# Six steps' banks and one eviction count in each word of TensorE's building table, with its waits at every sixth step

## The reference

```python
h = relu(layernorm(x)); x = x + attention(h)   # clip(qk[dst].qk[src]/8), softmax over dst, sum of v[src]
h = relu(layernorm(x)); x = x + conv(h)        # norm * segment_sum((h*norm)[src], dst) @ W + b
h = relu(layernorm(x)); x = x + edge_mlp(h)    # mlp([h[src], h[dst], edge_attr]) both ways, segment sums, mlp
h = relu(layernorm(x))
for _ in range(4):                             # x = x + the last feat
    a = segment_sum((einsum(feat, W) + b)[edge_type, src], dst); feat = gru_cell(a, feat)
```

## Time and profile before

| | |
|---|---|
| time, median of 3 runs | 13652.0 us (13648.86 to 13652.0) |
| profiled execution | 13654.69 us, its span 13653.0 us |
| busy share of the span | PE 81%, PEld 47%, DVE 41%, ACT 26%, POOL 32% |
| mean granted clock of TensorE | 0.892 |
| building, first to last matmul of L1139 | 317.0 to 2652.4 us |
| line L1139 on the chain that ended last | 11% of the span |
| L1139, 4859 matmuls | busy 1893.7 us, idle before 428.4 us, "issue" 212.9 of it |

### The profile page before, as it was taken

The page is one execution under the profiler, slowest core; times in us unless marked ns, Lnnn a source line. Parts: engine busy times, 40 slices in busy tenths (PEclk is TensorE's granted clock), DMA queues, the critical chain, the costliest instruction groups (busy, mean ns, idle before and its releaser), DMA issues.

```text
span 13653.0 us, 258090 instructions
## 1 busy us (share of the span) xinstructions
PE 11057.9 (81%) x60251; PEld 6361.4 (47%) x60252; DVE 5587.9 (41%) x21367; ACT 3529.7 (26%) x9549; POOL 4391.0 (32%) x3429
## 2 busy tenths in 40 slices
PE   2888888799976777777777777775899999999999
PEld 2444444333345555555555555554644444444443
DVE  6888888766624443443443443443311111111111
ACT  0666666533302222222222222222100000000000
POOL 2000000000005888888888888886000000000000
PEclk7666666699988999999999999998599999999999
DMA  2444444422262333333333333335399899899898
GB/s 99 139 136 139 139 136 140 139 87 93 87 273 36 42 42 42 42 42 42 42 42 42 42 42 42 42 42 35 109 354 348 338 348 348 337 349 348 338 349 306
DMA packets 1120492, 2096.55 MB, mean 154 GB/s; under 512 B 373090, under 2 KB 982915, under 8 KB 1012532
## 3 DMA queue, kind: packets, MB, share of 16 engines
q1 hardware_dynamic: 823768, 1913.47, 39.3%
q0 software_dynamic: 295904, 174.34, 12.0%
HBM read 1630.21 MB, written 457.17 MB: 153 GB/s over the span
## 4 chain that ended last, share of the span: by engine, by line
PE 54%; issue 19%; POOL 16%; DVE 4%; DMA 2%; ACT 1%; POOLq 1%; SPq 1%; DVEq 0%; ACTq 0%; another core or an unknown queue 0%
PE ps L1491 16%; PE ps L1139 11%; PE ps L1496 9%; POOL G L499 8%; POOL reverse L824 8%; PE ps L1194 4%; PE ps L1185 2%; DMA reverse<-SD,sidx 2%; DVE hots L1824 1%; PE ps L1294 1%; PE ps L1343 1%; PE ps L1354 1%; PE ps L1344 1%; POOLq L823 1%; PE ps L1357 1%
## 5 line engine op out<-in xcount | busy, mean ns | idle before, releaser
L824 POOL DMA_INDIRECT reverse<-SD,sidx x1660 | 2650.9, 1597 | 556.4 <-issue 496.2
L1491 PE MATMUL ps<-chunk,feat 128*128 128x512 f16 (+1 forms) x10192 | 2278.9, 375 | 14.8 <-DVE feat L2186 13.9
L499 POOL DMA_INDIRECT G<-h_table,idx x1660 | 1647.4, 992 | 1942.9 <-issue 1935.5
L1139 PE MATMUL ps<-hots 128*128 128x392 f16 x4859 | 1893.7, 449 | 428.4 <-issue 212.9
L1354 PE MATMUL ps<-MS,OH 128*128 128x128 f32 x3320 | 774.4, 316 | 1218.2 <-issue 811.9
L2023 DVE TENSOR_TENSOR acc<-acc,ps 128x132 f32 x1660 | 485.1, 292 | 3009.7 <-PE ps L1357 2958.5
L854 ACT ACTIVATE stagebuf<-ps 128x392 f32 x3248 | 1470.5, 506 | 884.5 <-PE ps L1142 804.8
L1491 PEld LDWEIGHTS ps<-chunk,feat 128*128 128x128 bf16 x10192 | 943.4, 98 | 1301.2 <-issue 307.8
L931 ACT ACTIVATE SD<-ps 128x129 f32<-128x129 f32 x1660 | 461.9, 278 | 3726.4 <-DMA reverse<-SD,sidx 3700.5
L1354 PEld LDWEIGHTS ps<-MS,OH 128*128 128x128 f32 x3320 | 542.8, 198 | 1771.6 <-issue 1748.7
L1343 PE MATMUL ps<-early,OT 128*128 128x256 f32 x3320 | 1081.3, 409 | 250.9 <-issue 225.8
(11 more groups left out here) (417 smaller groups left out, 14865.9 us busy)
## 6 DMA issues: line engine op xcount, KB each, us to landing
chunk<-adj SPq DMA_DIRECT2D x720, 1792.0 KB, 9.0
adj<-stagebuf SPq DMA_DIRECT2D x406, 784.0 KB, 5.3
chunkA<-adj SPq DMA_DIRECT2D x48, 1792.0 KB, 6.8
chunk<-adj SPq DMA_DIRECT2D x60, 1232.0 KB, 6.5
G<-in_edge SPq DMA_DIRECT2D x1660, 32.0 KB
G<-h_table,idx POOLq DMA_INDIRECT x1660
reverse<-SD,sidx POOLq DMA_INDIRECT x1660
reverse<-acc SPq DMA_DIRECT2D x4, 3225.0 KB, 20.0
```

The lines of the kernel that those rows point to most:

```text
L499: nc.gpsimd.indirect_dma_start(G[:, j, 0:width], None, table, bass.IndirectOffsetOnAxis(idx[:, j:j + 1], 0))\
L824: nc.gpsimd.indirect_dma_start(reverse[j % R], bass.IndirectOffsetOnAxis(sidx[:, j:j + 1], 0), SD[:, j % R, :], None, compute_op=ALU.add). ...
L1139: nc.tensor.matmul(ps[:, bass.ds(window % 8 * 512, 2 * COMBS)], hots[:, j // HG % HRING, 0:P, j % HG], hots[:, j // HG % HRING, P:P + 2 * ...
L1491: nc.tensor.matmul(bank[k % 2][:, 0:cols], feat[0][:, hi, 0:2, :].rearrange("p a d -> p (a d)"), columns(chunk4, i % DRING, m, cols), star ...
```

## The change

A word of the table now holds six steps' banks (18 bits) and above them one count of evictions (12 bits). A sweep of 64 steps has 11 words, ten of six steps and one of four, where it had 16. The table is 836 words long instead of 1216, and the words of sweep `it` begin at word 11 x `it` instead of 16 x `it`. TensorE's waits stand at every sixth step (before the steps 0, 6, ... 60 of a sweep) instead of at every fourth; the last group of a sweep has four steps. VectorE packs the new words in 15 operations. SyncE stores them with one transfer instead of two.

```diff
-VIRTW, BATCH = 16, 4
-PACK = 8
+VIRTW, BATCH = 16, 6
+BANKBITS = 3 * BATCH
...
-SWEEPW = 2 * SWEEP // PACK
+SWEEPW = -(-SWEEP // BATCH)
+WHOLE = SWEEP // BATCH
...
                 if j % BATCH == 0:
-                    free, odd = held["words"][SWEEPW // 2 + j // PACK], j // BATCH % 2
-                    pe.wait_ge(hot_made, min((k + BATCH) // HG, HGROUPS) if known(k) else it * (SWEEP // HG) + (j + BATCH) // HG)
-                    pe.wait_ge(evicted, (free >> 12) & 4095 if odd else free & 4095)
-                window = held["words"][j // PACK] >> 3 * (j % PACK)
+                    ready = min(j + BATCH, SWEEP)
+                    pe.wait_ge(hot_made, min((k - j + ready) // HG, HGROUPS) if known(k) else it * (SWEEP // HG) + ready // HG)
+                    pe.wait_ge(evicted, (held["words"][j // BATCH] >> BANKBITS) & 4095)
+                window = held["words"][j // BATCH] >> 3 * (j % BATCH)
...
-            link(copy_(pack_free, turned_free[:, :, BATCH - 1]))
-            link(both_(out=pack_free, in0=turned_free[:, :, PACK - 1], scalar=4096.0, in1=pack_free, op0=ALU.mult, op1=ALU.add))
-            link(copy_(pack_bank, turned_bank[:, :, 0]))
-            for i in range(1, PACK):
-                link(both_(out=pack_bank, in0=turned_bank[:, :, i], scalar=float(8 ** i), in1=pack_bank, op0=ALU.mult, op1=ALU.add))
...
+            copy_(need_word[:, :, 0:WHOLE], of_needed[:, :, :, BATCH - 1])
+            link(copy_(need_word[:, :, WHOLE], needed[:, :, SWEEP - 1]))
+            link(scalar_(need_word, need_word, BANKBITS, None, ALU.logical_shift_left))
+            copy_(word, of_banks[:, :, :, 0])
+            link(copy_(rest_word, banks[:, :, WHOLE * BATCH]))
+            for i in range(1, BATCH):
+                link(both_(out=word, in0=of_banks[:, :, :, i], scalar=float(8 ** i), in1=word, op0=ALU.mult, op1=ALU.add))
...
+            link(copy_(bank_word, packed[0:BC, :, :]))
+            tensor_(bank_word, bank_word, need_word, ALU.bitwise_or).then_inc(tab_copied, 1)
```

More of the change, by code:

```diff
@@ L179, in build @@
         key_table = dram("key_table", (TP, 3 * P))
-        step_rows = dram("step_rows", (BC, SWEEPS, 2, SWEEPW // 2), I32)
+        step_rows = dram("step_rows", (BC, SWEEPS * SWEEPW), I32)
         virt_rows = dram("virt_rows", (3 * VC, P), I32)
@@ L247, in build @@
         tabcols = here("tabcols", [P, 3 * BC])
-        packed = here("packed", [P, P // PACK])
+        packed = here("packed", [P, SWEEPS, SWEEPW])
         tabi = here("tabi", [P, P], I32)
@@ L611, in table @@
                 sp.dma_start(rows, tabi[0:rows.shape[0], :]).then_inc(tab_stored, 16)
-                sp.wait_ge(tab_stored, 16 * (n + 2))
+                sp.wait_ge(tab_stored, 16 * (n + 1))
                 lines = rows.rearrange("(q c) p -> q (c p)", q=count)
@@ L617, in _ @@
             sp.wait_ge(tab_copied, 1)
[L618 to L622, removed]
+            sp.dma_start(step_rows, tabi[0:BC, 0:SWEEPS * SWEEPW]).then_inc(tab_stored, 16)
+            sp.wait_ge(tab_stored, 16)
+            sp.dma_start(steptab[0:1, :], step_rows.rearrange("(o c) w -> o (c w)", o=1)).then_inc(tab_loaded, 16)
             table(1, virt_rows, 3, virttab, 32)
@@ L1126, in words @@
                     steptab[0:1, it * SWEEPW:(it + 1) * SWEEPW] if known(it) else steptab[0:1, bass.ds(it * SWEEPW, SWEEPW)],
-                    engines=(pe.engine,), min_val=0, max_val=max(8 ** PACK - 1, (VW + 8) * 4097),
+                    engines=(pe.engine,), min_val=0, max_val=(VW + PRE + 1 << BANKBITS) - 1,
                     skip_runtime_bounds_check_because="the path's tables are made of counts within these bounds")
@@ L1705, in _ @@
             v.wait_ge(tab_turned, 1)
-            turned_free, turned_bank = (bank[7][row:row + BC, 0:P].rearrange("c (w i) -> c w i", i=PACK) for row in (0, BROW))
-            pack_free, pack_bank = packed[0:BC, :], packed[BROW:BROW + BC, :]
-            link(copy_(pack_free, turned_free[:, :, BATCH - 1]))
-            link(both_(out=pack_free, in0=turned_free[:, :, PACK - 1], scalar=4096.0, in1=pack_free, op0=ALU.mult, op1=ALU.add))
-            link(copy_(pack_bank, turned_bank[:, :, 0]))
-            for i in range(1, PACK):
-                link(both_(out=pack_bank, in0=turned_bank[:, :, i], scalar=float(8 ** i), in1=pack_bank, op0=ALU.mult, op1=ALU.add))
-            link(copy_(tabi[0:BC, 0:P // PACK], pack_free))
-            copy_(tabi[BROW:BROW + BC, 0:P // PACK], pack_bank).then_inc(tab_copied, 1)
+            needed, banks = (bank[7][row:row + BC, 0:P].rearrange("c (s e) -> c s e", s=SWEEPS) for row in (0, BROW))
+            whole, last = slice(0, WHOLE * BATCH), SWEEP - WHOLE * BATCH
+            of_banks = banks[:, :, whole].rearrange("c s (w i) -> c s w i", i=BATCH)
+            of_needed = needed[:, :, whole].rearrange("c s (w i) -> c s w i", i=BATCH)
+            word, rest_word = packed[0:BC, :, 0:WHOLE], packed[0:BC, :, WHOLE]
+            bank_word = tabi[0:BC, 0:SWEEPS * SWEEPW].rearrange("c (s w) -> c s w", s=SWEEPS)
+            need_word = tabi[0:BC, P // 2:P // 2 + SWEEPS * SWEEPW].rearrange("c (s w) -> c s w", s=SWEEPS)
+            copy_(need_word[:, :, 0:WHOLE], of_needed[:, :, :, BATCH - 1])
[5 more added lines that the diff above has]
+                link(both_(out=word, in0=of_banks[:, :, :, i], scalar=float(8 ** i), in1=word, op0=ALU.mult, op1=ALU.add))
+            for i in range(1, last):
+                link(both_(out=rest_word, in0=banks[:, :, WHOLE * BATCH + i], scalar=float(8 ** i), in1=rest_word, op0=ALU.mult,
+                           op1=ALU.add))
+            link(copy_(bank_word, packed[0:BC, :, :]))
+            tensor_(bank_word, bank_word, need_word, ALU.bitwise_or).then_inc(tab_copied, 1)
             v.wait_ge(cmp_used, 3 * CG)
@@ L1759, in _ @@
             v.wait_ge(tab_turned, 2)
-            v.wait_ge(tab_stored, 32)
+            v.wait_ge(tab_stored, 16)
             copy_(tabi[0:3 * VC, :], bank[7][0:3 * VC, 0:P]).then_inc(tab_copied, 1)
@@ L1791, in _ @@
             v.wait_ge(tab_turned, 3)
-            v.wait_ge(tab_stored, 48)
+            v.wait_ge(tab_stored, 32)
             copy_(tabi[0:6, :], bank[7][0:6, 0:P]).then_inc(tab_copied, 1)
```

## The result

| | before | changed |
|---|---|---|
| time, median of 4 runs | 13652.0 us (13648.86 to 13658.5) | 13765.26 us (13754.72 to 13768.92) |
| ratio to before | | 1.008, 95% interval 1.0068 to 1.0093 |
| profiled execution, span | 13654.69 us, 13653.0 | 13754.72 us, 13753.0 |
| building, first to last matmul | 317.0 to 2652.4 us | 315.9 to 2759.3 us |

The changed kernel is 113 us slower, 0.8%. The forecast was 13867 us, 215 us slower: the sign and the cause came out as forecast, the size at half.

What follows compares the result with a forecast made beforehand. The prediction took TensorE's instruction sequencer, not its arithmetic, to bound the building. Its terms 4 + 198 + 12 + 1 gave +215 us on 13654.7, so 13870, forecast as 13867 us for the median; range 13660 to 13920.

Steps and rivals of the forecast that it cites:

- B: Rival on the table load: single words up to a 16-byte multiple, then fours; 5 accesses every sweep, 13705 us; chance 0.27.
- A: The forecast's own reading of the table load: fours only if it begins at a 16-byte multiple; 13820 to 13920 us; chance 0.50.
- Term 1: Group heads and inner steps in the building: fewer heads save 182 us, more and slower inner steps cost 185; +4 us.
- bits and place: Whether inner-step address instructions go by bits left above (heads and steps +4 us) or place in the group (-36 us).
- Term 2: TensorE's table load once a sweep: 9.5 accesses in the mean, 5.5 more than before, over 76 sweeps; +198 us.
- 1.9 for four accesses: Mean time in us taken for one table load of the kernel before, during the building; 0.475 us an access.
- 5.5 x 0.475: Table load's growth: 5.5 added accesses a sweep at the mean price of 0.475 us, 2.61 us a sweep.
- Term 3: TensorE's waits for evictions at every sixth step: 8 us over the last 112 windows, 4 in the body; +12 us.
- Term 4: Setup: VectorE's packing chain grows from 12 to 15 operations, SyncE's single store stays hidden; +1 us.
- C: Rival on the table load: price by started fours or nearly the same whatever its words; 13633 to 13665 us; chance 0.13.
- D: Rival on the table load: price by the word, five fewer save 45 us; 13624 us, or 13584; chance 0.08.
- about 200 ns a register: Skill page's price for the table load: five registers fewer save an estimated 1.0 us a sweep, -76 us; 13593 us.

Runs made afterwards that it cites:

- the single loads: Changed kernel with 14 kinds of table load, three of each, ahead of its building: eight words 0.591 us from a multiple of four, 1.941 from one past it.

## Why the prediction was right in sign and off in size

**The time.** 13765 us lies between B's 13705 and the range of A, and nearer to B. Only the loads' durations, not the time, show that A's reading of the load is the right one.

**What bounds the kernel.** Right. The matmuls got faster and the steps did not; the building's loss came out at the end to 0.1 us at the transfer of x.

**Term 1, heads and steps, +4 us forecast.** The heads within sweeps and the sweeps' starts came to -185 us with their waits, the inner steps to +171.4; without the 12 us of waits that is -26 us. Two small errors: the long head's 0.67 us was read from a head whose step has a shift of its own, and in the new table no head's step has one (0.648, and 759 x 0.022 = 17 us); and inner steps cost 0.389, not 0.393 (16 us). The choice between bits and place was right, and was shown.

**Term 2, the load, +198 us forecast, +122 measured.** This is the step that failed, in its size. The count of accesses was right: 11 single words in three sweeps of four and 5 accesses in the fourth, shown by the 1.32 and 2.64 us and by the single loads. The mean of a load before, "1.9 for four accesses", was right too (145.7 / 76 = 1.92). What failed is "5.5 x 0.475": it gives accesses that are added to a load the mean price of that load's accesses, though two fifths of this price (0.82 of 1.92 us) come from bursts of stores that last some 5 us. The quiet part of the growth is (2.31 - 1.10) x 76 = 92 us, by 0.22 us an access; bursts added 0.39 x 76 = 30 us, where the forecast's price held 0.2 us an access and so 84 us. That is 54 of the 76 us missed. The other 22 are in the quiet part: the forecast's price held 1.10 / 4 = 0.275 us an access, because it spread the load's fixed 0.1 us over four of them and took single words at the price of fours, where 0.22 was added for each.

**Term 3, the waits, +12 us forecast.** The heads take 28.7 us more than their medians would give in the changed kernel and 16.8 in the one before: +12. In the last stretch the waits for ScalarE grew from 8.6 us to 13.8, 5 us where I had 8, so the body has some 7 where I had 4.

**Term 4, setup.** VectorE's packing took 2.9 us for 2.5, and the building began 1.1 us earlier in this execution, not later. Nothing rests on it.

**Rivals.** B is refuted by eight words from one past a multiple at 1.94 us and by three sweeps of four at 2.63 us or more, C and D by the changed kernel's own loads, whose median more than doubled with five words fewer. The figure of about 200 ns a register (the Trainium skill, "Runtime: NRT & Kernel Launch", "Instruction fetch mechanics"), which the page gives with the register loads that the runtime puts in, is near what these loads from on-chip memory show for single words past a multiple, 0.23 to 0.24 us each, and far from aligned fours, 0.25 us for four registers; used for the difference of the two kernels it gives the wrong sign.

## What to carry to other kernels

Before packing a table of registers tighter, look at where each load begins: here 11 words from an address that is no multiple of 16 bytes cost 2.64 us when quiet, 12 from a multiple of it 0.855. Where a queue is bound by its issue, count its scalar instructions before its matmuls; a field that is read at each head belongs in the low bits: here that took heads from 0.648 to 0.570 us and made the last steps of a word shorter. And a mean price that holds a contention of limited length is good for another operation of the same kind, but not for making one operation longer.

## What the runs showed of the hardware

- TensorE's register load of 4 to 16 words costs 0.25 us for each four words where it begins at a multiple of 16 bytes, and 0.23 to 0.24 us for each word otherwise; it doesn't go over to fours at the next multiple (8 words from one past it 1.941 us), and an incomplete last four costs as much as single words (11 aligned words 1.322 us).
- During stores of 16 windows such a load costs up to 3.3 to 3.5 times as much (1.102 to 3.677 us, 0.844 to 2.925 us), and at most 3.5 us more in the two kernels whose loads are longest when quiet; doubled stores took the longest from 6.12 to 9.68 us.
- The first address instruction of a step on TensorE's sequencer takes 0.104 us without a shift, 0.130 to 0.139 us with one and 9 or more bits left, 0.119 to 0.127 us with 6 or 3 bits left (medians by the place in the word, over six kernels). A gain of 0.007 us an inner step was 28 us of the whole.
